# A two-layer adaLN transformer with experts: five engines' tables of steps rearranged, first norm, q and k projections, expert pieces and row sums

## The reference

```python
mod = (silu(c) @ wmod).reshape(32, 6, 1, -1)          # sa, ca, ga, sb, cb, gb
h = layernorm(x) * (1 + ca) + sa
x = x + ga * attention(h)                             # layer 0: ALiBi slopes, biases; layer 1: none
h = layernorm(x) * (1 + cb) + sb
x = x + gb * experts(h)                               # top 2 of 16, F = 64; layer 1: + shared, FS = 256

def attention(h):
    scores = einsum('bhqd,bhkd->bhqk', q, k) / sqrt(8) + slopes * dist
    return einsum('bhqk,bhkd->bhqd', softmax(scores), v) @ Wo.T + bo
def experts(x):                                       # layer 0; layer 1 is silu(x @ Wg) * (x @ Wu) @ Wd
    topk_w, topk_i = top_k(x @ router, 2); topk_w = softmax(topk_w)
    act = (clip(up, -7, 7) + 1) * gate * sigmoid(1.702 * gate)
    return sum over the two experts of weight * (act @ down + bias)
```

## Time and profile before

| | us |
|---|---|
| median of 3 runs (lowest to highest) | 1702.09 (1701.91 to 1704.56) |
| the profiled execution, its own time | 1702.93 |
| its span (first to last instruction) | 1701.2 |
| TensorE busy | 1354.3 |
| VectorE busy | 1300.5 |
| ScalarE busy | 1087.4 |
| GpSimd busy | 1012.4 |
| first scores of unit 0 | at 62.75 |
| maxima of unit 63, the last | end at 1479.5 |

### The profile page before, as it was taken

How to read it: one execution, slowest core, us unless ns; L and a number is a source line. 1 busy time by engine, 2 the same in 40 slices (tenths; PEclk the granted TensorE clock), 3 DMA queues, 4 the chain that set the end, 5 groups by cost and what they waited for, 6 DMA issues and landing times.

```text
span 1701.2 us, 45413 instructions
## 1 busy us (share of the span) xinstructions
PE 1354.3 (80%) x14409; PEld 836.5 (49%) x14409; DVE 1300.5 (76%) x3854; ACT 1087.4 (64%) x2558; POOL 1012.4 (60%) x1416
## 2 busy tenths in 40 slices
PE   2488888888888878888999889988889868875631
PEld 1144444445555545554556555655556535544531
DVE  5479998788887897879988898898988857743422
ACT  1188887677777776767777667776777656642321
POOL 1223334833585777577876678576865783686573
PEclk9999999899999998989999999999999989987766
DMA  3665766566677776776777667677667765656763
GB/s 90 151 149 150 161 151 144 139 157 160 173 187 176 176 174 175 184 170 166 188 170 177 152 162 183 166 186 175 170 181 188 181 177 142 176 166 172 214 196 100
DMA packets 447673, 283.04 MB, mean 166 GB/s; under 512 B 33773, under 2 KB 436751, under 8 KB 447439
## 3 DMA queue, kind: packets, MB, share of 16 engines
q1 hardware_dynamic: 412334, 237.12, 56.6%
q0 software_dynamic: 16384, 33.59, 7.1%
q10 hardware_dynamic: 18720, 9.44, 1.9%
HBM read 171.75 MB, written 108.18 MB: 165 GB/s over the span
## 4 chain that ended last, share of the span: by engine, by line
POOL 26%; PE 23%; DVE 23%; issue 17%; DMA 5%; ACT 3%; SPq 2%; POOLq 0%; DVEq 0%; ACTq 0%
DVE mx L1657 10%; POOL slot_dram L696 8%; POOL y_in L717 5%; PE ps_job L1109 5%; PE ps_s L1243 3%; PE ps_q L1082 3%; POOL ln_rs L662 2%; DMA k_stk<-part_dram 2%; DMA h_blk<-slot_dram 2%; POOL qk_part L743 2%; POOL qk_rest L739 2%; PE ps_q L1065 1%; POOL x L729 1%; PE ps_job L1130 1%; PE ps_q L1097 1%
## 5 line engine op out<-in xcount | busy, mean ns | idle before, releaser
L1657 DVE TENSOR_REDUCE mx<-ps_s 128x2 f32<-128x512 f32 x1024 | 655.2, 682 | 112.6 <-PE ps_s L1243 110.8
L894 ACT ACTIVATE prob<-ps_st 128x512 f32<-128x512 f32 x1024 | 557.1, 595 | 90.6 <-PE ps_st L1249 87.8
L1243 PE MATMUL ps_s<-k_stk,q_stk 51*128 51x256 bf16 x2048 | 361.0, 282 | 138.3 <-DVE mx L1657 68.3
L1249 PE MATMUL ps_st<-q_stk,k_stk 53*128 53x256 bf16 x2048 | 355.2, 281 | 6.6 <-ACT prob L894 6.3
L1109 PE MATMUL ps_job<-prob,v_ext 128*32 128x256 f32 x4096 | 291.1, 404 | 27.2 <-issue 10.0
L1243 PEld LDWEIGHTS ps_s<-k_stk,q_stk 51*128 51x128 bf16 x2048 | 141.6, 96 | 334.5 <-DVE mx L1657 198.5
L696 POOL DMA_INDIRECT slot_dram<-h_row,slot x256 | 255.8, 999 | 71.0 <-issue 65.4
L717 POOL DMA_INDIRECT y_in<-y_dram,slot x224 | 222.8, 995 | 77.6 <-issue 51.0
L836 ACT ACTIVATE o_sb<-ps_job 128x256 f32<-128x256 f32 x256 | 97.0, 379 | 173.0 <-PE ps_job L1109 169.0
L1109 PEld LDWEIGHTS ps_job<-prob,v_ext 128*32 128x32 f32 x4096 | 116.5, 113 | 131.6 <-issue 36.9
L739 POOL TENSOR_TENSOR qk_rest<-qk_f,qk_part 128x512 f32<-128x512 f32 x64 | 74.5, 1164 | 160.6 <-ACT qk_part L927 160.3
(11 more groups left out here) (206 smaller groups left out, 2642.2 us busy)
## 6 DMA issues: line engine op xcount, KB each, us to landing
w_q<-in_we SPq DMA_DIRECT2D x376, 128.0 KB
h_blk<-slot_dram SPq DMA_DIRECT2D x50, 512.0 KB, 5.2
part_dram<-qk_part SPq DMA_DIRECT2D x128, 192.0 KB
q_stk<-part_dram SPq DMA_DIRECT2D x128, 192.0 KB
k_stk<-part_dram SPq DMA_DIRECT2D x128, 192.0 KB
y_dram<-y_sb SPq DMA_DIRECT2D x46, 512.0 KB, 3.2
part_dram<-qk_part SPq DMA_DIRECT2D x128, 128.0 KB
mod_in<-row_dram SPq DMA_DIRECT2D x64, 192.0 KB
```

The source lines that it names most:

```text
L894: sc.activation(prob[:, (k ^ 1) % 8, :], ps_st[k % 2][:], ACT.Exp).then_inc(exp_done, 1)
L1243: mm = pe.matmul(ps_s[j % 2][:, t * S:(t + 1) * S], q_stk[us.tri][r0:r0 + R_BIAS, hp, t * P:(t + 1) * P], k_stk[us.tri][r0:r0 + R_BIAS, hp ...
L1249: mm = pe.matmul(ps_st[k % 2][:, t * S:(t + 1) * S], k_stk[ut.tri][r1:r1 + R_MAX, hp, t * P:(t + 1) * P], q_stk[ut.tri][r1:r1 + R_MAX, hp, ...
L1657: dve.tensor_reduce(mx[:, hp // 4, :, 4 * par + hp % 4], ps_s[j % 2][:].rearrange("p (t s) -> p t s", s=S), AX_X, ALU.max).then_inc(max_do ...
```

## The change

TensorE's table: the job h_t goes from place 5 (-27) to place 13 (-35), qk from place 9 (-23) to place 3 (-29). ScalarE, which reads JOBS too, follows; its xn goes from -33 to -38, its two qk_part copies from -22 and -19 to -28 and -25. GpSimd's two go from -21 and -18 to -27 and -24. VectorE's statistics of the first norm go from -43 to -42 and GpSimd's 1/std behind them from -42 to -41. SyncE's parts go from -17 to -20 and its set-up from SETUP + 4 = -10 to SETUP + 10 = -4, behind unit 0's stacks. Pieces of groups 0 to 3 start four steps earlier, of group 4 two later, of group 5 two later. Row sums of groups 0 to 4, with all that hangs on COMBINE, are one step later. h_t has four buffers instead of three, and one semaphore that h_t and ctx_t shared is two.

```diff
-        QUAD[last + 150 + 64 * (i // 3) + (0, 22, 42)[i % 3] if late < 0 else
-             END + (-106 + 16 * i, -8 + 12 * i, 56 + 8 * i, 112 + 8 * i)[late]] = PIECE_AT[g] + i
+        QUAD[last + (146, 152)[g >= SECOND] + 64 * (i // 3) + (0, 22, 42)[i % 3] if late < 0 else
+             END + (-104 + 16 * i, -8 + 12 * i, 56 + 8 * i, 112 + 8 * i)[late]] = PIECE_AT[g] + i
...
-        apart, lag = (2, 13) if late < 0 else (1, 9)
+        apart, lag = (2, 14) if late < 0 else (1, 9)
...
-        5: [("h_t", -27, 0), ("ctx_t", 53, S)], 6: [("max_t1", 22, 0), ("h2_t", 70, S)],
-        7: [("rank", 87, 0), ("owner", 103, P), ("sh_dn", 87, S)], 8: [("av2", 40, 0)], 9: [("qk", -23, 0)],
+        3: [("qk", -29, 0)], 5: [("ctx_t", 53, S)], 6: [("max_t1", 22, 0), ("h2_t", 70, S)],
+        7: [("rank", 87, 0), ("owner", 103, P), ("sh_dn", 87, S)], 8: [("av2", 40, 0)],
...
-        14: [("max_t0", 14, 0), ("v", 14, S)], 15: [("o_t0", 47, 0)]}
+        13: [("h_t", -35, 0)], 14: [("max_t0", 14, 0), ("v", 14, S)], 15: [("o_t0", 47, 0)]}
...
-                u = at(step, -17)
+                u = at(step, -20)
                 if u:
                     part_rows(u)
...
-                if step == SETUP + 4:
+                if step == SETUP + 10:
                     setup()
```

More of the change, by code:

```diff
@@ L233, in build @@
         xn = sb("xn", [P, TT, D])
-        h_t = [sb(f"h_t{i}", [P, S]) for i in range(3)]
+        h_t = [sb(f"h_t{i}", [P, S]) for i in range(4)]
         qk_f = sb("qk_f", [P, 2 * S])
@@ L345, in build @@
         ln_rstd = [sem("ln1_rstd"), sem("ln2_rstd")]
-        xn_ok, h_ctx_mm, h_ok = sem("xn_ok"), sem("h_ctx_mm"), sem("h_ok")
+        xn_ok, h_mm, ctx_mm, h_ok = sem("xn_ok"), sem("h_mm"), sem("ctx_mm"), sem("h_ok")
         qk_mm, qk_ok = sem("qk_mm"), sem("qk_ok")
@@ L394, in build @@
         S_DONE = UNITS * H
-        def h_turn(u):
-            return u.no + 1
-        def ctx_turn(u):
-            return u.no + (AT["ctx_t"] - AT["h_t"]) // H + 1
         def h2_turn(u):
@@ L721, in _ @@
             for step in range(FIRST, STEPS):
-                for i, after in ((0, -42), (1, 63)):
+                for i, after in ((0, -41), (1, 63)):
                     u = at(step, after)
@@ L735, in _ @@
                     pool.tensor_tensor(act[0], th_sb[0], u_sb[:], ALU.mult).then_inc(act0_ok, 1)
-                u = at(step, -21)
+                u = at(step, -27)
                 if u:
@@ L739, in _ @@
                     pool.tensor_tensor(qk_rest[:], qk_f[:], qk_part[:, 0, :], ALU.subtract).then_inc(qk_r, 1)
-                u = at(step, -18)
+                u = at(step, -24)
                 if u:
@@ L804, in norm_apply @@
                 if u.has(1):
-                    sc.wait_ge(h_ctx_mm, h_turn(u) - 1)
+                    sc.wait_ge(h_mm, u.no)
                 for t in range(TT):
@@ L821, in take_h @@
             def take_h(u):
-                sc.wait_ge(h_ctx_mm, h_turn(u))
+                sc.wait_ge(h_mm, u.no + 1)
                 if u.no == B:
                     sc.wait_ge(mod_ok, 4)
-                if u.has(3):
-                    sc.wait_ge(mxt0_v_mm, u.no - 2)
-                sc.activation(h_t[u.tri][:], ps_job[BANK["h_t"]][:, 0:S], ACT.Identity,
+                if u.has(4):
+                    sc.wait_ge(mxt0_v_mm, u.no - 3)
+                sc.activation(h_t[u.no % 4][:], ps_job[BANK["h_t"]][:, 0:S], ACT.Identity,
                               scale=mod[u.layer][:, 1, u.batch:u.batch + 1],
@@ L912, in rest @@
                         take_y(q, half)
-                u = at(step, -33)
+                u = at(step, -38)
                 if u:
@@ L921, in rest @@
                     take_qk(u)
-                u = at(step, -22)
+                u = at(step, -28)
                 if u:
@@ L927, in rest @@
                     sc.activation(qk_part[:, 0, :], qk_f[:], ACT.Copy).then_inc(qk_hi, 1)
-                u = at(step, -19)
+                u = at(step, -25)
                 if u:
@@ L947, in rest @@
                 if u:
-                    sc.wait_ge(h_ctx_mm, ctx_turn(u))
+                    sc.wait_ge(ctx_mm, u.no + 1)
                     if u.has(1):
@@ L1129, in project_qk @@
                 b = columns("qk")
-                pe.matmul(b[:, 0:S], wq[u.layer][:], h_t[u.tri][:], start=True, stop=True)
-                pe.matmul(b[:, S:2 * S], wk[u.layer][:], h_t[u.tri][:], start=True, stop=True).then_inc(qk_mm, 1)
+                pe.matmul(b[:, 0:S], wq[u.layer][:], h_t[u.no % 4][:], start=True, stop=True)
+                pe.matmul(b[:, S:2 * S], wk[u.layer][:], h_t[u.no % 4][:], start=True, stop=True).then_inc(qk_mm, 1)
             def project_v(u):
@@ L1135, in project_v @@
                 for t in range(TT):
-                    mm = pe.matmul(b[:, t * D:(t + 1) * D], h_t[u.tri][:, t * P:(t + 1) * P], wv[u.layer][:],
+                    mm = pe.matmul(b[:, t * D:(t + 1) * D], h_t[u.no % 4][:, t * P:(t + 1) * P], wv[u.layer][:],
                                    start=True, stop=True)
@@ L1280, in jobs @@
                 if "h_t" in units:
-                    mm = transpose_h(units["h_t"])
+                    transpose_h(units["h_t"]).then_inc(h_mm, 1)
                 if "ctx_t" in units:
-                    mm = transpose_ctx(units["ctx_t"])
-                if "h_t" in units or "ctx_t" in units:
-                    mm.then_inc(h_ctx_mm, 1)
+                    transpose_ctx(units["ctx_t"]).then_inc(ctx_mm, 1)
                 if "qk" in units:
@@ L1461, in normalise @@
                 if t == 0 and u.has(1):
-                    dve.wait_ge(h_ctx_mm, ctx_turn(u) - 1)
+                    dve.wait_ge(ctx_mm, u.no)
                 dve.tensor_tensor(ctx_sb[:, t, :].rearrange("p (h d) -> p h d", d=DH), o[:, :, 0:DH],
@@ L1711, in rest @@
                     owners(u)
-                u = at(step, -43)
+                u = at(step, -42)
                 if u:
```

## The result

| | us |
|---|---|
| before, median of 4 runs (lowest to highest) | 1702.00 (1699.47 to 1704.56) |
| changed, median of 4 runs | 1787.19 (1783.23 to 1787.54) |
| ratio, 95% interval | 1.0509 (1.0474 to 1.0544) |
| forecast, range | 1672 (1650 to 1704) |

The change is 85 us slower; the forecast was 30 us faster, and the time lies outside the range, beyond the slower rival's 1715 too. The profiled execution of the changed kernel took 1783.23 us, its span 1781.2.

The account below looks back on a forecast made before the run. No engine was full; the handshake of TensorE, VectorE and ScalarE in each pair (two loop steps) was taken to bound the kernel. Waits of -54 us, +22 coming back and +1 at the start gave -31: 1672 us, range 1650 to 1704.

Parts of the forecast that it names:

- slower rival: ScalarE's copies bunch in pairs 1 to 3, so scores wait for exponentials and TensorE falls behind: 1715 us, chance 0.15.
- Step 1: TensorE: h_t to pair 6 and qk to pair 1 spare VectorE waits for scores, -20 us (-40 to +15).
- Step 2: ScalarE: xn, h_t and qk copies move too, bunching in pairs 1 to 3; near nothing on average.
- Step 3: VectorE: first norm's statistics, moved to pair 3, fill its waits ahead of hot_rank, -18 us (-21 to 0).
- Step 4: GpSimd: qk work leaves the stretch ahead of the second norm's 1/std, shortening VectorE's waits, -8 us (-25 to +10).
- Step 5: Pieces of experts: gate products leave pair 5, ahead of att_tmp, -4 us (-8 to +4); earlier loads 0.
- Step 6: First twelve units, without pieces: the 1.21 us wait ahead of the maxima shrinks by 0.3 to 0.4 per unit, -4 us.
- Step 7: Start: unit 0 begins some 8 us earlier, then stands still while x loads late; +1 us (-3 to +8).
- All waits go: Rival: the handshake evens out and every wait taken becomes time; 1628 us at most, about 1650 at half, chance 0.10.
- Nothing on balance: Rival: the waits only move, to the maxima of pair 2 and to pair 7; 1702 us within 3, chance 0.09.

Follow-up runs that it names:

- e10_pieces_sums: The kernel before with only the pieces and the row sums moved; 1700.34 us, ratio 1.0018 to the kernel before.
- e11_setup_only: The kernel before with only set-up moved, from step -10 to -4, ahead of unit 1's parts; 1684.49 us, ratio 0.9922 to the kernel before.
- e5_layered: The changed kernel with the h_t and qk chain at new places in layer 0, old places in layer 1; 1801.13 us, ratio 0.9849 to the kernel before.
- e9_layered_setup: Same as e5_layered, with set-up one step earlier, ahead of unit 1's parts; 1685.42 us, ratio 0.9917 to the kernel before.

## Why the prediction was wrong

**Step 1, the failed one.** It said that "Pair 1 held only two bursts of scores and the o_t1 transposes, so it mostly fits". That counts what a pair has to *do*; it does not ask which bank the job writes and who reads that bank before it. The kernel's description says that a job waits until the job before it in its bank is read, and JOBS with VectorE's steps 77 and 83 tell the rest: sh1 is read one pair after it is written, behind two maxima (1.28 us) and a piece's product; a job one pair behind it must stand. The term was -20 us with +15 as its worst; units 36 to 62 alone made it +85. In the 74 us of the middle stretch TensorE's waits for the bank are 69.9, and its busy time, with the clock at its lower level for 78.5 us more, is 22.5 longer; other waits shrank. The sum had no term for either. The sign that the prediction named for this step, VectorE's wait for scores down from 61.4 us to about 35, came out as 112.3 over the same units. What the step said of layer 0 holds in direction: the wait for scores in units 12 to 35 fell from 48.0 us to 31.2. VectorE's waits there, the changed kernel, 264 to 787 us:

```profile
DVE mx L1649 <- PE ps_s L1237: 31.2, 46, 1.7
DVE att_tmp L1675 <- PE ps_job L1168: 22.3, 11, 5.8
DVE h_mid L1421 <- POOL ln_rs L656: 8.9, 7, 1.9
DVE den_r L1451 <- PE ps_job L1111: 5.6, 7, 2.4
DVE ln_st L1411 <- POOL x L723: 4.8, 4, 1.9
DVE hot_rank L1512 <- PE ps_job L1183: 2.7, 6, 1.1
```

Before, 264 to 792 us, these were 48.0, 10.8, 14.4, 0.9, 0.3 and for both kinds of hot_rank 5.8. The waits for scores, 1/std and hot_rank fell by 25.2 us; att_tmp, den_r and ln_st rose by 20.7. With the stretch shorter by 5 us, that is nearly the whole account: the waits moved.

**Step 2, ScalarE's bunch.** Right that it is near nothing. In the changed kernel, 787 to 1335 us, TensorE waits for exponentials 0.9 us in 2; before it was 7.1. The slower rival named this bunch as its mechanism, so the rival was wrong in mechanism as well as in size, though its sign came true. ScalarE's waits for GpSimd, which could have driven it, are 6.5 us in units 12 to 55 (dz 3.5, ln_shift 3.0).

**Step 3, statistics and hot_rank.** Half right: hot_rank's waits went from 17.8 us to 2.7 + 0.2 + 8.1 over the same units, where I had named under 5 (my 15.6 were the two kinds of the earlier trace rows and left out a third of 2.2), and in the last eight from 13.7 to 4.2.

**Step 4, GpSimd.** The waits for 1/std fell from 24.8 us to 10.1 in the same units, more than the 8 I took. As time nothing of it is seen in layer 1, where TensorE is late for another reason.

**Step 5, pieces.** I took -4 for the gate products; e10_pieces_sums gives +3 (from -2 to +8): nothing. att_tmp's waits in layer 0 rose rather than fell.

**Step 6, the first twelve units.** Units 4 to 11 took 16.90 us each against 17.19: -2.3 us, under the 17.1 that I had named.

**Step 7, the start.** Right. I had the rest of x at 59.8 and the scores of unit 1 at 78.6; they came at 60.45 and 79.32. The first maxima came at 56.5 (near 55 forecast) and the stand ahead of unit 1 was 9.7 us (8), and unit 4 is 2.6 us later where I had +1. VectorE at unit 0's and unit 1's first maxima:

```profile
56.52 2.69 DVE L1649 TENSOR_REDUCE mx<-ps_s 128x2 f32<-128x512 f32 x4 [8.27 <-PE ps_s L1237]
...
79.97 1.29 DVE L1649 TENSOR_REDUCE mx<-ps_s 128x2 f32<-128x512 f32 x2 [9.74 <-PE ps_s L1237]
```

The step also contained the way to the 13 us: only the stores of unit 1's parts, in the same step of SyncE's program, kept set-up back. The Trainium skill (DMA: Bandwidth & Descriptors, Queues, rings and completion order) has descriptors taken in ring order. The traces agree, though they do not show the rings themselves. In the changed kernel, with the rest of x issued 10.7 us ahead of unit 1's stacks, the scores come 8.2 us behind the stacks' issue (71.13 to 79.32); in e11_setup_only, with 15.9 us between, 6.4 us (59.87 to 66.22). Of the 13.1 us between the two kernels at unit 1's first maxima (79.97 and 66.86) the larger part is the issue itself, 11.3 us later.

**The sum and the rivals.** With the old places in layer 1, e5_layered came to -1.5%, 29 us, in a slower round, near the forecast's -30, though that forecast was for the new places in both layers; and in the round of 1698 us e9_layered_setup, with the earlier set-up in it besides, came to only -12 us, no more than set-up alone. There, and in the change itself, layer 0's part of the forecast (step 6's -4 and nearly all of step 1's -20) mostly did not show as time: units 4 to 35 gained 8.7 us of the 24 in the change. In the slower rounds it did, by 17 to 29 us. "All waits go" is out. "Nothing on balance" is nearest for layer 0 in the rounds of 1698 and 1702 us. The 0.15 that I gave to slower stood on the wrong mechanism; the right one could be read from JOBS and the steps of `shared_act` alone.

## What to carry to other kernels

When a job moves in a hand-ordered pipeline, list for its new place the buffer it writes, the reader of the job before it there, and what that reader's engine does first; a gap of one period is a wait if the reader acts behind its own main work. Do it for every kind of stage: here layer 0 was free and layer 1 paid. Adding up loads per slot finds none of this, and neither do busy times: VectorE's, ScalarE's and GpSimd's stayed within 1% while the time rose by 5%. And price such a wait above its own length, since here the clock that TensorE was granted fell behind 15 of 38 such stands.
